# Moving the second attention layer's mask arithmetic from VectorE to GpSimd, between the issues of the mask loads

## The reference

```python
h = relu(layernorm(x)); x = x + L0(h, adj)      # (adj @ h) @ W + b
h = relu(layernorm(x)); x = x + L1(h, adj)      # adj scaled by degrees
h = relu(layernorm(x)); x = x + L2(h, adj)      # attention, 8 heads of 32
h = relu(layernorm(x)); x = x + L3(h, adj)      # attention, 8 heads of 32
```

```python
scores = scores + (1.0 - adj)[None, None, :, :] * -1000000000.0
```

## Time and profile before

| what | value |
|---|---|
| median of 3 executions | 2866.49 us (2864.7 to 2868.12) |
| profiled execution, its own time | 2864.98 us |
| span of the profiled execution | 2862.8 us |
| TensorE busy | 2809.5 us (98%) |
| VectorE busy | 2319.6 us (81%) |
| ScalarE busy | 2175.3 us (76%) |
| GpSimd busy | 590.0 us (21%) |

### The profile page before, as it was taken

One profiled execution on the slowest core, in us unless ns is written; L12 is line 12 of the kernel. 1 busy time (PEld: TensorE's weight loads), 2 busy tenths in 40 slices (PEclk: granted clock), 3 DMA queues, 4 the chain that ended last, 5 costly groups with the idle time before them and its releaser, 6 DMA issues.

```text
span 2862.8 us, 59796 instructions
## 1 busy us (share of the span) xinstructions
PE 2809.5 (98%) x23872; PEld 2257.2 (79%) x23872; DVE 2319.6 (81%) x4293; ACT 2175.3 (76%) x3926; POOL 590.0 (21%) x538
## 2 busy tenths in 40 slices
PE   7999998999999999999999999999999999999998
PEld 6888887677878787878787878777878777877776
DVE  6866765888888888888888888888888888888876
ACT  3000001889898989898989889898989898989897
POOL 2222221011414141414141415010101010101000
PEclk9999999999999999999999999999999999999999
DMA  3001002323242423333333352323333333323332
GB/s 129 30 30 60 30 30 54 89 60 93 65 100 57 98 66 93 71 92 72 86 78 86 78 144 71 91 66 88 76 86 78 85 79 77 80 70 85 74 75 64
DMA packets 123587, 217.18 MB, mean 76 GB/s; under 512 B 20016, under 2 KB 88240, under 8 KB 123312
## 3 DMA queue, kind: packets, MB, share of 16 engines
q1 hardware_dynamic: 122160, 209.14, 29.4%
q0 software_dynamic: 1152, 4.19, 0.5%
HBM read 53.87 MB, written 25.17 MB: 28 GB/s over the span
## 4 chain that ended last, share of the span: by engine, by line
PE 79%; DVE 2%; ACT 1%; DMA 0%; issue 0%; SPq 0%; ACTq 0%; DVEq 0%
PE t_ring_ps L749 32%; PE t_ot_ps L777 16%; PE t_s_ps L736 16%; PE t_ring_ps L719 4%; PE t_ring_ps L721 4%; PE t_ring_ps L720 4%; PE t_ring_ps L794 1%; DVE t_T L1008 1%; PE t_ring_ps L798 1%; DVE t_PT L1085 1%; PE t_ring_ps L813 0%; DVE t_hT_lo L1020 0%; DMA t_k<-t_st_lo 0%; ACT t_PT L927 0%; ACT t_T L921 0%
## 5 line engine op out<-in xcount | busy, mean ns | idle before, releaser
L1008 DVE CUSTOM_DVE_ANT_0 t_T<-t_s_ps,mask 128x1024 f32<-128x1024 f32 x1024 | 1239.4, 1215 | 55.2 <-PE t_s_ps L736 53.6
L921 ACT ACTIVATE t_T<-t_T,t_low 128x1024 f32<-128x1024 f32 x1024 | 1175.8, 1152 | 59.6 <-DVE t_low L1008 59.5
L749 PEld LDWEIGHTS t_ring_ps<-t_ident,t_T 128*128 128x128 f32 x8192 | 936.5, 141 | 225.0 <-issue 80.3
L749 PE MATMUL t_ring_ps<-t_ident,t_T 128*128 128x128 f32 x8192 | 1102.9, 275 | 9.1 <-DVE t_hT_lo L1020 4.7
L927 ACT ACTIVATE t_PT<-t_ring_ps 128x512 f32<-128x512 f32 x1456 | 812.6, 597 | 114.1 <-PE t_ring_ps L749 93.3
L736 PE MATMUL t_s_ps<-t_k,t_q 128*128 128x512 f32 x2048 | 722.1, 433 | 6.1 <-DMA t_k<-t_st_lo 4.2
L1085 DVE COPY t_PT<-t_ring_ps 128x512 f32<-128x512 f32 x592 | 408.8, 691 | 144.1 <-PE t_ring_ps L749 140.5
L777 PE MATMUL t_ot_ps<-t_PT,shared 128*32 128x256 f32 x8192 | 494.9, 382 | 0.3 <-ACT t_PT L927 0.3
L777 PEld LDWEIGHTS t_ot_ps<-t_PT,shared 128*32 128x32 f32 x8192 | 240.0, 109 | 224.6 <-issue 68.7
L247 ACT ACTIVATE g_yT_hi<-g_ps 128x512 fp32r<-128x512 f32 x64 | 38.3, 598 | 401.3 <-PE g_ps L187 401.3
L736 PEld LDWEIGHTS t_s_ps<-t_k,t_q 128*128 128x128 f32 x2048 | 315.7, 191 | 15.3 <-DMA t_k<-t_st_lo 4.7
(11 more groups left out here) (154 smaller groups left out, 3149.3 us busy)
## 6 DMA issues: line engine op xcount, KB each, us to landing
t_q<-t_st_hi SPq DMA_DIRECT2D x256, 128.0 KB, 2.4
t_k<-t_st_hi SPq DMA_DIRECT2D x256, 128.0 KB, 2.4
t_k<-t_st_lo SPq DMA_DIRECT2D x256, 128.0 KB, 2.5
t_q<-t_st_lo SPq DMA_DIRECT2D x256, 128.0 KB, 2.4
shared<-x_after_graph_layers SPq DMA_DIRECT2D x8, 1024.0 KB, 6.3
t_xe<-x_after_graph_layers SPq DMA_DIRECT2D x32, 256.0 KB, 3.1
x_after_layer<-t_xe SPq DMA_DIRECT2D x32, 256.0 KB, 2.1
shared<-x_after_layer SPq DMA_DIRECT2D x8, 1024.0 KB, 6.6
```

The costliest lines, as they stand in the source:

```text
L749: last = nc.tensor.transpose(banks[b][:, i * P:(i + 1) * P], T[u % RING][:, kt * P:(kt + 1) * P], ident[:])
L921: nc.scalar.activation(T[u % RING][:], T[u % RING][:], ACT.Exp, bias=low[:, u % RING:u % RING + 1], scale=-1.0, accum_out=rsum[:, u:u + 1] ...
L1008: nc.vector.tensor_tensor_reduce(out=T[u % RING][:], in0=s_ps[u % 2][:], in1=mask[:, qt, :], scale=1.0, scalar=3.4e38, op0=ALU.add, op1=AL ...
```

## The change

The function `mask3` moves from VectorE's list to GpSimd's. It is called from `load_mask3`: after the load of tile `t` has been issued, GpSimd computes tile `t - 2`, and the last two tiles after the last load. VectorE keeps its wait on `mask3_done`. The value products in groups of four key tiles are in both kernels.

```diff
@@ VectorE, masked
                 if job == B and u < NT:
 
-                    mask3(qt)
                     dve.wait_ge(mask3_done, qt + 1)
@@ VectorE
-            def mask3(t):
-
-                dve.wait_ge(mask_in[t], 16)
-                nc.vector.tensor_scalar(mask[:, t, :], mask[:, t, :], 1.0, -1.0e9, ALU.subtract, ALU.mult)\
-                    .then_inc(mask3_done, 1)
@@ GpSimd
+            def mask3(t):
+
+                pool.wait_ge(mask_in[t], 16)
+                nc.gpsimd.tensor_scalar(mask[:, t, :], mask[:, t, :], 1.0, -1.0e9, ALU.subtract, ALU.mult)\
+                    .then_inc(mask3_done, 1)
+
             def load_mask3():
 
                 for t in range(NT):
                     pool.wait_ge(t_done, UNITS * (B - 1) + UNITS - NT + t + 1)
                     pool.dma_start(mask[:, t, :], a["adj"][t * P:(t + 1) * P, :]).then_inc(mask_in[t], 16)
+                    if t >= 2:
+                        mask3(t - 2)
+                for t in range(NT - 2, NT):
+                    mask3(t)
```

## The result

The changed kernel takes 2871.55 us (median of 20 executions, 2868.74 to 2876.83) against 2865.51 us before (20 executions, 2862.75 to 2868.66). The ratio is 1.002, with a 95% interval of 1.0013 to 1.0026. It is slower by 6.0 us, where 2.3 us of gain were forecast, and the time lies above the range.

The account below looks back on a forecast made before the run. TensorE was taken as the bound, with a DMA and VectorE delaying the passage by 4.91 us. 3.2 us removed less 0.9 us for late tiles gave 2.3 us gained: 2866.49 to 2864.2 us, 8-in-10 range 2861.0 to 2868.6 us.

Parts of the forecast that it names:

- What bounds the kernel, and the ceiling: Passage from job 7 to job 8: mask loads and arithmetic together cost 4.91 us, the most any repair can give.
- What the change removes: At the passage, eight VectorE instructions, 5.8 us of its time, worth 3.2 us at the end.
- What it adds: Eight one-input operations of 128 by 1024 on GpSimd, taken at 1.1 us each, upper bound 2.6 us.
- What it moves: Loads 4 to 7 issue later behind GpSimd's waits; tiles 6 and 7 1.6 us late, costing 0.9 us.
- 3.2 reached the end (55%): Of 5.8 us VectorE was late at the passage, 3.2 reached the end; so 1.6 us late becomes 0.9 us.
- second rival: Loads 5 to 7 take 12.2 to 13.7 us again; 2.4 us slower, 2868.9 us; chance 0.18.
- The head-0 stall: Scores of unit 64 wait for head 0's operands at the passage; 1.7 us, expected to stay as it is.
- What stands behind GpSimd's list: Job 8's `move_v` waits until 1692.2 us, 1.3 us later; head 2's loads keep 3.0 us of room, no cost.
- the late issues are paid in full: The second rival: late loads 5 to 7 land as slowly as before; 2868.9 us, chance 0.18, 0.04 beyond 0.2%.
- GpSimd at work slows VectorE: Rival: eight masked adds at double length put back more than was taken; 2869 us or so, chance 0.04.

Follow-up runs that it names:

- no_arithmetic: Kernel before with the arithmetic of layer L3's mask left out; VectorE only waits for each tile's load: 2861.83 us, ratio 0.9992.
- add_mult: Changed kernel with GpSimd's instruction written as add -1, then multiply by -1e9: 2864.82 us, ratio 0.9993 to the kernel before.
- multiply_alone: Changed kernel with GpSimd only multiplying by -1e9, the subtraction left out: 2868.69 us, ratio 1.0003 to the kernel before.
- add_mult_loads_first: Changed kernel with add -1, then multiply by -1e9, and all eight loads issued before the first tile is computed: 2863.52 us, ratio 0.999 to the kernel before.
- mult_add: Changed kernel with GpSimd's instruction written as multiply by -1e9, then add 1e9: 2863.74 us, ratio 0.9992 to the kernel before.

## Why the prediction was wrong

**What bounds the kernel, and the ceiling.** Right. The 4.91 us of the earlier trace rows are all due to the mask: without loads and arithmetic 0.01 us stay. They were split into 1.7 us for head 0's operands and 3.2 us for VectorE; no_arithmetic takes away 3.67 us and leaves 1.24, within what the wait for head 0 varies from run to run.

**What the change removes.** Right. VectorE's busy time in the three groups is that of an ordinary job.

**What it adds.** This is the step that failed: "I take 1.1 us, as the second ALU step is the only difference", with 2.6 us as the upper bound. It measured 3.63 us, above even the upper bound, and tile 7 was ready at 1698.4 us where 1692.2 had been forecast. The same arithmetic in the cheap form (add_mult) brings the passage from 9.99 back to 1.92 us, so this price is what the change lost by. Price and bounds came from rows of a copy, of a two-input operation and of VectorE, and not from rows of the same instruction on GpSimd. Such rows were there, small ones; GpSimd's groups of the kernel before, by form:

```profile
L1204 POOL TENSOR_SCALAR t_var<-t_mv 128x2 f32<-128x2 f32 x32 | 7.1, 221 | 318.6 <-DVE t_mv L1072 318.6
L259 POOL TENSOR_SCALAR g_var_eps<-g_mv 128x8 f32<-128x8 f32 x16 | 3.8, 240 | 273.3 <-DVE g_mv L306 273.3
L1180 POOL TENSOR_SCALAR t_var_eps<-t_mv 128x8 f32<-128x8 f32 x15 | 3.7, 249 | 180.8 <-DVE t_mv L1102 180.8
```

Six more elements take 19 to 28 ns more, 3.2 to 4.7 ns each, so that 1024 would take an estimated 3.5 to 5.0 us. A copy of 1024 in 1.04 us is 1 ns each. It is a rough slope from very small sizes, and the form there is an add alone, measured later at 2.78 us; that its lower end lies near 3.63 us is chance. But it would have shown that the copy is no safe stand-in. In the Trainium skill, GPSIMD Engine Reference, section 3.1, bodies of up to two operations per element are put at about 1.03 cycles each, at the 1.2 GHz of that reference an estimated 0.88 us for 1024 elements. The pairs of add and multiply come near it (1.05 us in all, and 0.43 us between 512 and 1024 elements); subtract and multiply differs, 3.63 us.

**What it moves.** The wait in front of each issue was costed with a cheap operation, at 1.6 us of lateness. With the cheap form the passage costs 1.06 and 1.92 us in two runs, where 149.2 - 146.6 = 2.6 us were forecast. That this is near is partly luck: the forecast was 1.7 us for head 0 and 0.9 us for a late tile, and in these runs TensorE waits at most 0.3 us for head 0, while unit 71 is 1.2 and 1.9 us late. With the dear one, GpSimd's own work sets the pace: 8 x 3.63 us and five issues fill 32.9 us, and no load is waited for. The step "3.2 reached the end (55%)" was wrong too. The 5.8 us are VectorE's work, not its lateness: the kernel before had unit 71 late by 5.1 us in all, some 1.7 of it from head 0, and nearly all of it reached the end. So does the lateness of the last tile in the other runs (10.1 us for a cost of 9.99, 1.9 for 1.92). The prediction's own second rival passed lateness on whole.

**The head-0 stall** was left as it was in the sum. In the changed kernel it is gone: the groups at unit 60 start at 1670.41 and the next at 1677.78, an ordinary 7.37 us. But paced loads left 0.6 us of it in one run, loads spaced by GpSimd's work 1.5 us in another (multiply_alone), and all loads at once 0.5 us in a third (add_mult_loads_first). What decides it stays open.

**What stands behind GpSimd's list.** The copy `move_v` ran 7.5 us later than in the earlier trace rows, and the loads of head 2 with it. No wait for them shows, as TensorE was late too.

**The rivals.** The slower one, "the late issues are paid in full", came nearest in time, 2868.9 us and 2872.8 us with GpSimd at 2.6 us a tile, but for another reason: it wanted loads 5 to 7 to take 12.2 to 13.7 us again, and they took 4.0 to 7.7 us. It put the point at which 0.2% is passed at a tile 8.9 us late; 10.1 us gave a ratio of 1.002. That GpSimd at work slows VectorE is refuted: with GpSimd busy 31.37 of 32.14 us, VectorE's masked adds from 1670 to 1705 us took 1221 ns on average, and no add of the whole execution over 1227 ns, as before.

The changed kernel's 5.1 us more at the passage are less than the 6.0 us between the medians. The two profiled executions are only 4.2 us apart (2869.17 and 2864.98 us), the changed one 2.4 us under its median. Where the rest comes from is open; the last section has one candidate.

## What to carry to other kernels

An instruction that moves to another engine is to be priced by that instruction with its own operations on that engine: at one shape the same instruction took from 1.03 to 3.67 us here, and a row of another instruction of the right shape gave neither a value nor a bound. Tiny rows of the same instruction give a rough slope, which is a warning and not a price. Where the engine has a cheap way and a dear way to say the same arithmetic, try them side by side in one run before the schedule is judged: here subtract 1 against add -1 was worth 8.1 us, more than the 4.91 us that the passage had cost. When a consumer takes tiles at a fixed pace, compare the producer's total with the deadline of the last tile first; that lateness arrived at the end undiminished here.

## What the runs showed of the hardware

**GpSimd's tensor_scalar has very different prices.** On 128 by 1024 elements in place: pairs of add and multiply 1.03 to 1.06 us, one step alone 2.76 to 2.82 us, pairs with subtract or maximum 3.62 to 3.67 us. Two steps can be cheaper than one. The changed kernel, mult_add, add_mult and multiply_alone have eight instructions each of their form, which agree within 0.06 us; the other forms were timed in one execution, on one tile each.

**TensorE's clock fell inside the passage.** Windows of the changed kernel (length, PE busy, granted clock, DMA):

```profile
1684.00:1690.00 6.00, 3.51 (x28) 0.88 0.94 316
1690.00:1696.00 6.00, 4.27 (x38) 0.84 0.01 4
```

The same window of the kernel before, where TensorE had lost less:

```profile
1690.00:1696.00 6.00, 5.40 (x46) 1.00 0.38 106
```

One entry of TensorE's timeline in the changed kernel:

```profile
1688.65 3.55 PE L777 MATMUL t_ot_ps<-t_PT,shared 128*32 128x256 f32 x32
```

And one in multiply_alone, where eight such transposes take 1.04 us before the passage:

```profile
1695.43 1.94 PE L749 MATMUL t_ring_ps<-t_ident,t_T 128*128 128x128 f32 x8
```

After TensorE had stood idle for 0.2, 0.5 and 1.95 us, the 32 value products at 1688.65 took 3.55 us instead of 1.93, so part of the stretch was at 1.2 GHz instead of 2.4. In multiply_alone it had waited 0.9 and 2.2 us before the entry shown. In the changed kernel's execution this slower stretch cost nothing to speak of: the passage costs 9.99 us where unit 71 was 10.1 us late.

The 20 executions of the changed kernel are roughly ordered by the mean clock: the fastest, 2868.7 to 2870.5 us, have 0.995 to 0.996, the slowest, 2875.5 and 2876.8 us, have 0.992. But the kernel before shows the same order: of its 27 executions beside add_mult, nine at 0.996 have a mean of 2864.6 us and two at 0.993 one of 2870.9 us. So time and clock vary together in both kernels, and no run shows that the waits at the passage lower the clock in more executions. That this makes the 6.0 us between the medians out of the 5.1 us at the passage is possible, but was not tested.
